# Attention: the transposes of an earlier tile's mixed probabilities placed between the two halves of a tile's scores

## What is computed

```python
qe = einsum('hbtd,hde->hbte', q, Wq_exp)      # 6 expanded queries per token
ke = einsum('hbtd,hde->hbte', k, Wk_exp)
qe, ke, ve = qe * mask, ke * mask, ve * mask  # 2 shared experts, 2 chosen of the other 4
attn = softmax(einsum('rbqhd,rbkhd->rbhqk', qe, ke) / D ** 0.5)
o = einsum('rbhqk,rbkhd->rbqhd', attn, ve)
o = einsum('rbthd,rbth->bthd', o, rw)         # weighted by the router
```

## Time and profile before

| | us |
|---|---|
| median of 3 runs | 2622.17 |
| lowest and highest | 2619.18, 2627.49 |
| the profiled execution, its own time | 2620.94 |
| its span | 2619.2 |
| attention's score maxima, first to last start on DVE | 368.57 to 1029.35 |
| PE, DVE, ACT, POOL busy over the whole span | 90%, 61%, 44%, 48% |

### The profile page before, as it was taken

The page is one execution under the profiler, slowest core; times in us unless marked ns, Lnnn a source line. Parts: engine busy times, 40 slices in busy tenths (PEclk is TensorE's granted clock), DMA queues, the critical chain, the costliest instruction groups (busy, mean ns, idle before and its releaser), DMA issues. The chain is left out here.

```text
span 2619.2 us, 34298 instructions
## 1 busy us (share of the span) xinstructions
PE 2359.1 (90%) x9812; PEld 1590.8 (61%) x9812; DVE 1606.0 (61%) x2464; ACT 1140.9 (44%) x2390; POOL 1255.3 (48%) x1189
## 2 busy tenths in 40 slices
PE   7999979999999998798999994679899877999999
PEld 6788845555555554684888882435445325788877
DVE  4240239999999998585222224679999986411253
ACT  2333029999999997223222223632223113311121
POOL 1012035666666663566645323179999984111110
PEclk9999989999999998888999996789999998999999
DMA  5245435565555653776434314544444446101022
GB/s 181 83 135 183 121 99 160 165 175 164 166 166 166 170 171 129 210 222 222 145 116 155 107 49 151 199 155 168 174 162 179 172 151 181 65 25 48 16 89 65
DMA packets 264547, 370.58 MB, mean 141 GB/s; under 512 B 33528, under 2 KB 116488, under 8 KB 264432
## 3 DMA queue, kind: packets, MB, share of 16 engines
q1 hardware_dynamic: 228496, 301.25, 36.9%
q0 software_dynamic: 11040, 36.64, 4.2%
q10 hardware_dynamic: 24896, 31.24, 3.4%
HBM read 255.09 MB, written 113.98 MB: 141 GB/s over the span
## 5 line engine op out<-in xcount | busy, mean ns | idle before, releaser
L1082 ACT ACTIVATE attn_probs<-attn_ps_score,attn_nmax 128x512 f32<-128x512 f32 x512 | 343.2, 675 | 2.3 <-DVE attn_nmax L1156 2.3
L2711 PE MATMUL scan_ps_o<-scan_qs,scan_sel 128*128 128x512 f32 x512 | 280.9, 639 | 62.6 <-DVE scan_qs L2652 55.7
L2669 DVE TENSOR_TENSOR_SCAN scan_st<-scan_ps_dec,scan_kv 128x512 f32<-128x512 f32 x256 | 305.9, 1209 | 11.6 <-POOL scan_kv L2618 11.6
L989 PE MATMUL attn_ps_score<-attn_KK,attn_X 64*128 64x512 f32 x512 | 214.5, 465 | 21.3 <-ACT attn_probs L1082 20.9
L1170 DVE SCALAR_TENSOR_TENSOR attn_mixed<-attn_probs,attn_cf,attn_mixed 128x512 f32<-128x512 f32 x256 | 194.4, 759 | 9.1
L2711 PEld LDWEIGHTS scan_ps_o<-scan_qs,scan_sel 128*128 128x128 f32 x512 | 90.7, 197 | 167.1 <-DVE scan_qs L2652 103.1
L2618 POOL TENSOR_TENSOR scan_kv<-gla_vb,gla_gk 128x512 f32<-128x512 f32 x128 | 160.7, 1276 | 40.8 <-POOLq L2139 34.5
L1145 DVE TENSOR_REDUCE attn_raw<-attn_ps_score 128x2 f32<-128x1024 f32 x128 | 156.4, 1222 | 27.1 <-PE attn_ps_score L989 26.0
L989 PE MATMUL attn_ps_score<-attn_KL,attn_X 64*128 64x512 f32 x512 | 172.9, 422 | 0.0
L989 PE MATMUL attn_ps_score<-attn_KK,attn_Y 64*128 64x512 f32 x512 | 160.0, 397 | 1.0 <-POOL attn_Y L879 1.0
L2618 POOL TENSOR_TENSOR scan_kv<-gla_vb,scan_gk 128x512 f32<-128x512 f32 x128 | 159.2, 1273 | 2.4 <-DVE scan_st L2669 2.4
(11 more groups left out here) (559 smaller groups left out, 6440.2 us busy)
## 6 DMA issues: line engine op xcount, KB each, us to landing
gla_vb<-gv SPq DMA_DIRECT2D x256, 256.0 KB
rows_x<-attn_zeros SPq DMA_DIRECT2D x32, 1024.0 KB, 13.5
late<-rows SPq DMA_DIRECT2D x32, 384.0 KB, 9.0
attn_spread<-rows SPq DMA_DIRECT2D x32, 384.0 KB, 9.1
moe_raw<-in_L_ffn_gating POOLq DMA_DIRECT2D x6, 2048.0 KB, 9.6
moe_xb<-rows_x SPq DMA_DIRECT2D x39, 256.0 KB, 2.8
rows_y<-moe_y ACTq DMA_DIRECT2D x39, 256.0 KB, 2.0
sg<-proj_tile SPq DMA_DIRECT2D x32, 256.0 KB, 2.0
```

The source lines that it names most:

```text
L989: last = nc.tensor.matmul(ps_score[n][:, j, :], weights, y[p][half, :], start=(r == 0), stop=(r == len(terms) - 1))
L1082: nc.scalar.activation(probs[b][:, at_j, :], ps_score[n][:, j, :], ACT.Exp, bias=nmax[b][:, at_j:at_j + 1], accum_out=Z[b][:, at_j:at_j + ...
L2669: V.tensor_tensor_scan(st[r][:, :], ps_dec[n % 2][:, :], kv[r][:, :], 0.0, ALU.mult, ALU.add).then_inc(st_ready, 1)
L2711: nc.tensor.matmul(ps_o[w][:, :], sel[:, P - GPH - GPH * d:2 * P - GPH - GPH * d], qs[i % RING][:, :], start=(d == 0), stop=(d == HALF - 1 ...
```

## The change

`scores` takes one more argument, `between`. After the matmuls of the chosen experts it calls `turn` with it, and then goes on to the matmuls of the shared experts. `step` no longer calls `turn` after `scores`. The number of instructions on each engine is the same, and no wait is added or taken away: `turn` has its two waits at the new place.

```diff
-            def scores(i, p, u, t, first):
+            def scores(i, p, u, t, first, between=None):
...
                     last.then_inc(qk_done, 1)
+                    if n == AB and between is not None:
+                        turn(*between)
...
-                scores(i, p, u, 0, first)
-                if not first:
-                    turn(bu, 2, False)
+                scores(i, p, u, 0, first, None if first else (bu, 2, False))
...
-                scores(i, p, u, 1, first)
-                if not first:
-                    turn(bu, 3, False)
+                scores(i, p, u, 1, first, None if first else (bu, 3, False))
...
-                scores(i, p, u, 2, first)
-                turn(u, 0, first)
+                scores(i, p, u, 2, first, (u, 0, first))
...
-                scores(i, p, u, 3, first)
-                turn(u, 1, first)
+                scores(i, p, u, 3, first, (u, 1, first))
```

## The result

| | us |
|---|---|
| kernel before, median of 4 runs beside the change | 2620.68 (2617.16 to 2627.49) |
| changed kernel, median of 4 runs | 2663.02 (2660.71 to 2666.65) |
| ratio (the two medians alone give 1.0162) | 1.0177, 95% interval 1.0158 to 1.0197 |
| span of the profiled execution, before and after | 2619.2, 2663.1 |

The change makes the kernel slower, by 1.6 to 2.0%, 41 to 52 us. The span grew by 43.9 us. All of it lies in attention: from the first to the last read of the chosen scores it is now 1072.62 - 366.07 = 706.6 us, against 660.8 before, +45.8.

What follows compares the result with a forecast made beforehand. DVE was taken to bound attention. The two-tile loop, 4.14 + 1.53 + 3.48 + 1.70 = 10.85 us, gave 5.43 a tile against 5.13, so 125 x 0.30 = 37.5 us and about 2660 us, range 2638 to 2686.

Steps and rivals of the forecast that it cites:

- The bound and the margin: DVE bounds attention without idle time; shared scores come 0.46 us and chosen scores 0.17 us before DVE reads them.
- Which wait binds: At the new place transposes wait for ACT's copy of tile n-3, ending 706.40, later than the mixture, 705.85.
- The loop over two tiles: From `cf` through ACT's copy, transposes, shared scores and DVE to `cf` two tiles later: 10.85 us, 5.43 a tile.
- the stagger of the halves: On PE, shared scores took 0.96 us because their halves were released one after the other; without that, 0.86.
- the 3.48: DVE from reading the shared maxima to the next tile's chosen maxima: 3.43 us in one tile, taken as 3.48.
- The sum: In attention +0.30 us a tile over 125 tiles, 37.5 us, all reaching the kernel's end: about 2660 us.
- The mixture's loop: Mixture's end, transposes, shared scores, DVE: 1.53 us against 1.55, costing about nothing.
- Rival A: Transposes fill PE's waits for ACT's exponentials: free, 2622 us, or a gain to 2615; chance 0.10.
- Rival B: PE's idle time in attention lowers its clock: 2683 us if one tile in four falls, range 2670 to 2755; chance 0.12.
- The transpose's price: Four transposes on PE take 0.49 us together; at about 275 ns each, 1.1 us and +75 us.
- Shares: Signs of a right forecast in attention: DVE's busy share near 92%, PE's near 90%.

Runs made afterwards that it cites:

- ACT's new order at the old place: Kernel before, with ACT's copy out of the transpose bank moved ahead of the shared exponentials and the transposes left behind the shared scores: 2624.62 us, ratio 1.0024.
- the run with the waits alone: Changed kernel with only the transposes' two waits between chosen and shared scores, all four transposes behind both: 2631.17 us, ratio 1.0043.
- the swap: Kernel before, with POOL's gating of the output and its masked query swapped in the third tile of a unit: 2622.3 us, ratio 1.0012.

## Why the prediction was right, point by point

- **The bound and the margin.** DVE had its shared scores 0.46 us early, and the doubled transposes at the old place confirm that PE was not the bound, though 96% busy. For the chosen scores the prediction chose an unusual tile. They were 0.17 us early there, but in most tiles they come just in time, as in the next one, where they end at 710.79 and are read at 710.83:

```profile
710.17 0.62 PE L989 MATMUL attn_ps_score<-attn_KK,attn_Y 64*128 64x512 f32 x2
```

  The idle column hides such a wait. A read of the chosen scores that waits for nothing starts 0.08 us before the mixture ahead of it ends, as all 97 do in the steady part of the changed kernel; here it starts 0.03 before. In 57 of 97 steady tiles before, DVE waited in this way for the chosen scores, by 0.02 to 0.06 us. They bound those tiles as closely as DVE's own work did. The forecast doesn't hang on this, but that DVE never waits was not so.
- **Which wait binds.** The prediction said ACT's copy of tile n-3, and not the mixture. With the copy moved, the ratio falls from 1.0177 to 1.0023, and ACT's new order at the old place gives 1.0024; this is shown.
- **The loop over two tiles.** It was put at 10.85 us, and measured 10.95 in the mean. Its shape is shown too: neighbouring tiles alternate, 5.26 and 5.66 in the ones above, and the loop follows the number of transposes in a straight line.
- **Sizes that were off.** The transposes take 0.56 us to the next matmul there, not 0.49: in the row they start on an engine that stands idle. The shared scores take 0.97, not 0.86. I took 0.86 from a tile in which they followed the chosen scores without a break; behind other work, or behind a wait alone (700.35 to 700.68 in the run with the waits alone), the first pair of matmuls takes 0.33 us instead of 0.23, here 710.45 to 710.78. Why was not tested. I had named the stagger of the halves as the cause of the 0.96 before, and it was not; the halves now start together. Against these stands 3.37 on DVE in place of 3.48: the 3.48 held the 0.05 us of waiting for the chosen scores, which in the changed kernel end 0.14 us or more before they are read, and the mean of the tiles that POOL slows, which are now fewer. Terms too small by 0.19 us in all and terms too large by 0.13 met in one sum; that it came out 0.06 off (10.85 against 10.91) is in part luck.
- **The sum.** +0.30 a tile was forecast and +0.34 measured; 37.5 us against 43.9 in the span. Predicted 2660, measured 2663.0.
- **The other loops.** The mixture's loop was said to close at 1.53 us against 1.55; it takes 1.68 where it is free to show itself, against 1.60 in an ordinary tile. So it was not slack, and by itself costs 0.07 us a tile.
- **Rival A, free or faster.** It falls for the second of the reasons given, that the copy stands behind the shared exponentials. The first, that DVE had nothing to give back, was nearly so.
- **Rival B, the clock.** PE is now idle before the transposes for 0.6 to 0.95 us in nearly every tile, and the granted clock stayed at 1.00 in the steady part. The swings that the Trainium skill tells of ("TensorE: Matmul & The Clock Gate", "A second HAM failure mode: psum-queue depth-cycling") don't occur here at this idle time.
- **The transpose's price.** Four between the scores cost 0.43 us of the loop, 0.11 each. About 275 ns each, the figure of the Trainium skill ("TensorE: Matmul & The Clock Gate", Part 4: PE-mode transpose), is how long one of them takes (288 ns in the mean here), not what it adds to a row of them.
- **Shares.** PE's share fell to 85%, not about 90; DVE's to 90.6, near the 92 said.

## What to carry to other kernels

Idle time in front of a waiting matmul is not a free place: work moved into it brings its own waits, and an engine in order makes everything behind it wait for them too. Before moving a step, write down when each of its waits is met and what stands right behind the new place, and close the loop over as many tiles as it spans; here one line of ACT's order decided between a loss of 0.2% and one of 1.8%. And ask what the moved step reads, its DMAs too: that omission cost 1.5% on POOL.

## What I had not expected

- PE at 97.9% busy with 0.4 us more work a tile and no time lost that can be told: pairs of 64-row matmuls, released together, made up 0.30 us for it (1.19 against 1.49 us for the eight chosen ones), and 0.12 came off the time between their end and DVE's read.
- DVE's mixture became faster while DVE was made to wait. The mean of its first operation from 470 to 970 us fell from 838 to 770 ns:

```profile
L1170 DVE SCALAR_TENSOR_TENSOR attn_mixed<-attn_probs,attn_cf 128x512 f32<-128x512 f32 x97 | 81.2, 838 | 0.0
```

```profile
L1166 DVE SCALAR_TENSOR_TENSOR attn_mixed<-attn_probs,attn_cf 128x512 f32<-128x512 f32 x92 | 70.8, 770 | 0.0
```

  The first row is of the kernel before, the second of the changed one. What the changed one avoids is POOL. Here is a mixture of the kernel before that is hit:

```profile
717.93 1.27 POOL L895 TENSOR_TENSOR attn_masked<-late 128x512 f32<-128x512 f32 x1 [0.36 <-DVE attn_nmax L1156]
```

```profile
718.72 1.04 DVE L1170 SCALAR_TENSOR_TENSOR attn_mixed<-attn_probs,attn_cf 128x512 f32<-128x512 f32 x1
```

  POOL's operation ends at 719.20 and DVE's 0.55 us later. There is no exception in the traces: over 96 tiles the kernel before has 39 mixture operations of more than 0.8 us, and each ends 0.54 to 0.55 us after the end of a 128x512 operation of POOL, as do the 12 of the changed kernel, the 62 of the run with POOL's operation moved and the 37 of the swap. It holds for four different operations of POOL, and in the two runs that moved one, the stretch moved with it. The Trainium skill ("SBUF — State Buffer", its table of terms) says that DVE and GpSimd share a pair of ports, and that the loser is fully blocked for the other's whole instruction. These durations agree: the stretch grows one for one with the overlap.
